# A three-layer conv/attention/expert kernel: DVE's address read, SyncE's bulk loads, V's place and attention's chunk stages are reordered

## The reference

```
x = x + moe0(groupnorm(x))      # 8 experts, top 2; gelu(x w1 + b1) w2 + b2 per expert, and a shared gated FFN
t = t + attention(layernorm(t)) # 12 heads of 16 channels per image
t = t + moe1(layernorm(t))      # 16 experts, top 2; silu(x wg) * (x wu) wd, and a shared one

# attention, per image and head (256 x 256):
att = softmax(q k^T / 4)
att = softmax(att * mask)       # mask 0.5 where row % 64 == column % 64, else 1
out = (att v) w_out + b_out
```

## Time and profile before

| | |
|---|---|
| median of the runs shown | 509.32 us |
| profiled execution | 508.83 us, span 507.0 us, mean granted PE clock 0.97 |
| PE / DVE / ACT / POOL busy | 455.0 / 225.8 / 158.4 / 125.4 us |
| layer 0: routing and shared FFN, expert loop, sums | to 56, 56 to 157, 157 to 181 us |
| Q, K, V; attention; tail and routing | 181 to 211, 211 to 324, 324 to 362 us |
| layer 1's expert loop; sums and output | 362 to 492, 492 to 507 us |
| chain that ended last | PE 76%, DVE 8%, DMA 7%, issue 4% |

### The profile page before, as it was taken

How to read it: one execution, slowest core, us unless ns; L and a number is a source line. 1 busy time by engine, 2 the same in 40 slices (tenths; PEclk the granted TensorE clock), 3 DMA queues, 4 the chain that set the end, 5 groups by cost and what they waited for, 6 DMA issues and landing times.

```text
span 507.0 us, 7727 instructions
## 1 busy us (share of the span) xinstructions
PE 455.0 (90%) x2395; PEld 327.7 (65%) x2396; DVE 225.8 (45%) x597; ACT 158.4 (31%) x394; POOL 125.4 (25%) x136
## 2 busy tenths in 40 slices
PE   0999889999998598799999997799899999999996
PEld 0755456666668587777676766555577777777775
DVE  4465142222221475367878794545253333333322
ACT  2024312121221033348768683312222222222210
POOL 3201144454442000000000000000335455544430
PEclk9999989999999899579999999899999999999999
DMA  8997001111001980000000038093001101110006
GB/s 235 250 340 204 16 25 40 40 34 37 28 16 55 307 346 2 0 1 0 1 3 1 1 77 204 1 258 84 18 25 30 31 26 31 33 37 20 0 2 186
DMA packets 18057, 38.64 MB, mean 76 GB/s; under 512 B 4420, under 2 KB 13892, under 8 KB 17586
## 3 DMA queue, kind: packets, MB, share of 16 engines
q1 hardware_dynamic: 10610, 30.45, 21.0%
q0 software_dynamic: 5280, 6.32, 4.4%
q10 hardware_dynamic: 2144, 1.57, 1.0%
HBM read 35.16 MB, written 7.67 MB: 84 GB/s over the span
## 4 chain that ended last, share of the span: by engine, by line
PE 76%; DVE 8%; DMA 7%; issue 4%; ACT 2%; DVEq 1%; POOL 1%; POOLq 0%; ACTq 0%; SPq 0%
PE bank L1174 16%; PE bank L1189 12%; PE bank L1110 10%; PE bank L1168 5%; PE bank L1359 5%; DVE scratch L995 4%; PE bank L1354 4%; PE bank L1181 3%; PE bank L1312 3%; DMA w_first<-y_rows 3%; PE bank L1150 2%; DMA rows<-xn_rows,slot_tok 2%; PE bank L1096 2%; PE bank L1373 2%; PE bank L1341 2%
## 5 line engine op out<-in xcount | busy, mean ns | idle before, releaser
L1174 PE MATMUL bank<-w_first,rows_t 96*128 x248 | 85.4, 487 | 0.8 <-ACT rows_t L587 0.6
L502 POOL DMA_INDIRECT y_rows<-y,slot_row x54 | 55.4, 1025 | 108.2 <-DVE y L871 58.4
L494 POOL DMA_INDIRECT rows<-xn_rows,slot_tok x56 | 57.4, 1025 | 94.1 <-DVE slot_tok L821 36.9
L1189 PE MATMUL bank<-w_second,hid_t 128*128 x370 | 70.8, 331 | 7.6 <-issue 3.9
L1189 PEld LDWEIGHTS bank<-w_second,hid_t 128*128 128x128 f32 x370 | 59.1, 191 | 10.6 <-issue 10.5
L1174 PEld LDWEIGHTS bank<-w_first,rows_t 96*128 96x128 f32 x248 | 44.6, 190 | 26.2 <-issue 1.5
L655 ACT ACTIVATE scratch<-bank,neg_max 128x256 f32<-128x256 f32 x96 | 44.2, 481 | 8.4 <-PE bank L1341 7.5
L863 DVE TENSOR_TENSOR act_h<-bank,act_g 128x384 f32<-128x384 f32 x31 | 17.3, 557 | 63.8 <-PE bank L1174 63.8
L1168 PE MATMUL bank<-w_first,rows_t 96*128 (+1 forms) x92 | 44.3, 603 | 1.1 <-issue 1.0
L540 POOL COPY act_h<-o_inv 128x256 f32<-128x256 f32 x12 | 4.8, 403 | 154.6 <-DVE o_inv L1005 154.6
L995 DVE SCALAR_TENSOR_TENSOR scratch<-scratch,exp_inv,const 128x256 f32<-128x256 f32 x96 | 41.4, 492 | 0.8
(11 more groups left out here) (175 smaller groups left out, 658.5 us busy)
## 6 DMA issues: line engine op xcount, KB each, us to landing
w_first<-in_gate_up SPq DMA_DIRECT2D x16, 576.0 KB, 11.0
w_second<-in_down SPq DMA_DIRECT2D x1, 4608.0 KB, 25.9
w_first<-in_fc SPq DMA_DIRECT2D x1, 3072.0 KB
w_second<-in_fc SPq DMA_DIRECT2D x1, 3072.0 KB, 28.5
xn_rows<-xn_tok SPq DMA_DIRECT2D x2, 768.0 KB, 10.0
rows<-xn_rows,slot_tok POOLq DMA_INDIRECT x56, 2.6
y_rows<-y,slot_row POOLq DMA_INDIRECT x54, 2.3
w_first<-in_x_t SPq DMA_DIRECT2D x2, 384.0 KB, 5.0
```

What stands on the lines that cost most here:

```text
L494: pool.indirect_dma_start(rows[b % 2][:], None, xn_rows[L.l], bass.IndirectOffsetOnAxis(slot_tok[:, b:b + 1].bitcast(U32), 0), bounds_chec ...
L502: pool.indirect_dma_start(y_rows[L.l], bass.IndirectOffsetOnAxis(slot_row[:, b:b + 1].bitcast(U32), 0), y[b % 2][:], None, bounds_check=TO ...
L1174: ins = pe.matmul(bank[:, 5 + g, 0:I1], rows_t[0:CH, k, :], w(CH, (k * 2 + g) * I1, I1), start=(k == 0), stop=(k == NCH - 1))
L1189: ins = pe.matmul(bank[:, 1, 0:C], hid_t[:, tile(ic)], w(P, ic * C, C), start=(ic == 0), stop=(ic == L.IC - 1))
```

## The change

Four orders change; no arithmetic does.

1. `result`: layer 0's bias address is read into its register ahead of the waits for `y_ps` and `scattered`.
2. SP waits for both parts of both returned rows of layer 0 (`y_in[0]`, `y_in[1]`) before it issues `wo`, the gate/up weights and `down`, instead of for layer 0's last product.
3. PE computes V ahead of the scores of pairs 0 and 1, and waits for Q's and K's parts only behind it; DVE copies V ahead of the two row maxima.
4. In attention the chunk stages of PE stand ahead of `att_transpose(p)`, behind the wait for `p2_ready`, in the order spread, values, sums, project, at lags 3, 1, 2 and 4. Fillers: 2 for pairs 0 to 2, then 1, and none in a step with values or project. ACT's and DVE's loops have 28 steps, and PE's 24 with four more written out, so the last chunks take the same path; on DVE `residual` comes last in a step and `out_norm` and `invert_sums` ahead of `neg_maximum`. In the 4 steps behind the last pair PE has the normalization's transposes and the shared FFN between the stages, and 5 fillers. The shared FFN's (1, 1) moves from `plan[1]` ahead of the second logits, (1, 0) ahead of the second transposes.

The diff, cut to its core:

```diff
+        VALUES, SUMS, SPREAD, PROJECT = 1, 2, 3, 4
+
         def chunk_at(p, lag):
             c = (p - lag + 1) // PAIRS_CHUNK - 1
-            if c == N_CHUNKS - 1 or (p - lag + 1) % PAIRS_CHUNK or c < 0 or c >= N_CHUNKS:
-                return None
-            return c
+            return None if (p - lag + 1) % PAIRS_CHUNK or c < 0 or c >= N_CHUNKS else c
+
+        def image_at(p):
+            c = chunk_at(p, PROJECT)
+            return c // HC if c is not None and c % HC == HC - 1 else None
+
+        STEPS = range(N_PAIRS + PROJECT)
...
-            1: ([(1, 1), (2, 0), "count", (2, 1), "rank", (3, 0), "expert", (3, 1), (4, 0), (4, 1), (5, 0), "slots",
+            1: ([(2, 0), "count", (2, 1), "rank", (3, 0), "expert", (3, 1), (4, 0), (4, 1), (5, 0), "slots",
...
             bring_back(sp, L0, 0)
-            sp.wait_ge(L0.y_ps, NB0)
+            for s in L0.y_in[0:2]:
+                sp.wait_ge(s, 16 * TOPK)
             sp.dma_start(wo, d["wo"]).then_inc(s_attw, 16)
...
-            for p in range(N_PAIRS):
+            for p in STEPS:
                 if p + 2 < N_PAIRS:
                     exp_scores(p + 2)
-                exp_att(p)
-                if chunk_at(p, 1) is not None:
-                    out_copy(chunk_at(p, 1))
-            out_copy(N_CHUNKS - 1)
+                if chunk_at(p, VALUES) is not None:
+                    out_copy(chunk_at(p, VALUES))
+                if p < N_PAIRS:
+                    exp_att(p)
...
             def result(L, b, u, turn):
+                if L.l == 0:
+                    at = dve.value_load(blk_weights[0:1, 2, bass.ds(b, 1)], min_val=0, max_val=(E0 - 1) * C)
                 dve.wait_ge(L.y_ps, b + 1)
...
-            neg_maximum(0)
-            neg_maximum(1)
             dve.wait_ge(filled, 1)
             for n in range(NT // 2):
                 dve.wait_ge(v_ps, n + 1)
...
+            neg_maximum(0)
+            neg_maximum(1)
...
-            for p in range(N_PAIRS):
-                if p == 0:
-                    neg_maximum(2)
-                if (chunk_at(p, 5) or 0) % HC == HC - 1:
-                    residual(chunk_at(p, 5) // HC)
-                attention(p)
+            neg_maximum(2)
+            for p in STEPS:
+                if p < N_PAIRS:
+                    attention(p)
+                if p == N_PAIRS:
+                    ln_stats(0)
+                if p == N_PAIRS + 2:
+                    ln_rows(2, 0)
+                if chunk_at(p, SUMS) is not None:
+                    invert_sums(chunk_at(p, SUMS))
+                if chunk_at(p, SPREAD) is not None:
+                    out_norm(chunk_at(p, SPREAD))
                 if p + 3 < N_PAIRS:
                     neg_maximum(p + 3)
-                if chunk_at(p, 2) is not None:
-                    invert_sums(chunk_at(p, 2))
-                if chunk_at(p, 3) is not None:
-                    out_norm(chunk_at(p, 3))
...
+                if image_at(p) is not None:
+                    residual(image_at(p))
...
-            pe.wait_ge(parts_ready, 2 * QKC)
-            scores(0)
-            scores(1)
             for n in range(NT // 2):
...
                 ins.then_inc(v_ps, 1)
+            pe.wait_ge(parts_ready, 2 * QKC)
+            scores(0)
+            scores(1)
             pe.wait_ge(v_out, NT // 2)

             def att_transpose(p):
-                if p:
-                    pe.wait_ge(p2_ready, p)
-                for _ in range(2 if p else 8):
-                    pe.matmul(bank[:, 4, 0:TOKENS_IMG], ident, mask, start=True, stop=True)
                 pe.wait_ge(att_ready, p + 1)
...
+            def chunk_stages(p):
+                if p:
+                    pe.wait_ge(p2_ready, min(p, N_PAIRS))
+                stages = ((SPREAD, spread_inverses), (VALUES, weigh_values), (SUMS, sums_by_token))
+                for lag, stage_of in stages:
+                    if chunk_at(p, lag) is not None:
+                        stage_of(chunk_at(p, lag))
+                if image_at(p) is not None:
+                    project(image_at(p))
+
+            def keep_busy(n):
+                for _ in range(n):
+                    pe.matmul(bank[:, 4, 0:TOKENS_IMG], ident, mask, start=True, stop=True)
+
+            scores(2)
             for p in range(N_PAIRS):
-                if p == 0:
-                    scores(2)
                 if p + 3 < N_PAIRS:
                     scores(p + 3)
+                chunk_stages(p)
+                if chunk_at(p, VALUES) is None and image_at(p) is None:
+                    keep_busy(2 if p < 3 else 1)
                 att_transpose(p)
-                if chunk_at(p, 2) is not None:
-                    sums_by_token(chunk_at(p, 2))
-                if chunk_at(p, 3) is not None:
-                    spread_inverses(chunk_at(p, 3))
-                if (chunk_at(p, 4) or 0) % HC == HC - 1:
-                    project(chunk_at(p, 4) // HC)
-                if chunk_at(p, 1) is not None:
-                    weigh_values(chunk_at(p, 1))
...
+            chunk_stages(N_PAIRS)
+            keep_busy(2)
+            chunk_stages(N_PAIRS + 1)
+            keep_busy(2)
             norm_transposes(2, 0)
+            chunk_stages(N_PAIRS + 2)
+            keep_busy(1)
             pe.wait_ge(tp_out, NT + 2)
             pe.wait_ge(s_sh1, 32)
             shared(L1, 0, 0)
+            chunk_stages(N_PAIRS + 3)
             shared(L1, 0, 1)
...
+            shared(L1, 1, 0)

             pe.wait_ge(x_new, IMAGES)
             norm_transposes(2, 1)
-            shared(L1, 1, 0)
+            shared(L1, 1, 1)
```

More of the change, by code:

```diff
@@ L872, in result @@
                 else:
-                    at = dve.value_load(blk_weights[0:1, 2, bass.ds(b, 1)], min_val=0, max_val=(E0 - 1) * C)
                     ins = v.tensor_tensor(y[u][:], bank[:, 1, 0:C], fc2_b[:, bass.ds(at, C)], ALU.add)
@@ L1021, in residual @@
                 dve.sem_inc(x_new, 1)
-            for p in range(N_PAIRS):
-                if p == 0:
-                    neg_maximum(2)
-                if (chunk_at(p, 5) or 0) % HC == HC - 1:
-                    residual(chunk_at(p, 5) // HC)
-                attention(p)
+            neg_maximum(2)
[10 more added lines that the diff above has]
+                    out_norm(chunk_at(p, SPREAD))
                 if p + 3 < N_PAIRS:
                     neg_maximum(p + 3)
-                if chunk_at(p, 2) is not None:
-                    invert_sums(chunk_at(p, 2))
-                if chunk_at(p, 3) is not None:
-                    out_norm(chunk_at(p, 3))
-            ln_stats(0)
-            out_norm(N_CHUNKS - 2)
-            invert_sums(N_CHUNKS - 1)
-            ln_rows(2, 0)
-            out_norm(N_CHUNKS - 1)
-            residual(IMAGES - 1)
+                if image_at(p) is not None:
+                    residual(image_at(p))
             ln_stats(1)
@@ L1407, in project @@
                 ins.then_inc(proj_ps, 1)
+            def chunk_stages(p):
[11 more added lines that the diff above has]
+            scores(2)
             for p in range(N_PAIRS):
-                if p == 0:
-                    scores(2)
                 if p + 3 < N_PAIRS:
                     scores(p + 3)
+                chunk_stages(p)
+                if chunk_at(p, VALUES) is None and image_at(p) is None:
+                    keep_busy(2 if p < 3 else 1)
                 att_transpose(p)
-                if chunk_at(p, 2) is not None:
-                    sums_by_token(chunk_at(p, 2))
-                if chunk_at(p, 3) is not None:
-                    spread_inverses(chunk_at(p, 3))
-                if (chunk_at(p, 4) or 0) % HC == HC - 1:
-                    project(chunk_at(p, 4) // HC)
-                if chunk_at(p, 1) is not None:
-                    weigh_values(chunk_at(p, 1))
-            weigh_values(N_CHUNKS - 1)
-            spread_inverses(N_CHUNKS - 2)
-            sums_by_token(N_CHUNKS - 1)
-            spread_inverses(N_CHUNKS - 1)
-            project(IMAGES - 1)
+            chunk_stages(N_PAIRS)
+            keep_busy(2)
+            chunk_stages(N_PAIRS + 1)
+            keep_busy(2)
             norm_transposes(2, 0)
+            chunk_stages(N_PAIRS + 2)
+            keep_busy(1)
             pe.wait_ge(tp_out, NT + 2)
```

## The result

The changed kernel takes 480.28 us (median of 4 runs, 476.89 to 484.92; the kernel before 509.27 beside it), a ratio of 0.942 with a 95% interval of 0.934 to 0.950. The forecast was 483.1. The profiled execution took 480.29 us, its span is 478.5 us. The kernel's four runs differ by the clock that they were granted (mean 0.985 in the fastest, 0.975 in the two in the middle, 0.968 in the slowest), so I compare stretches of traces more than medians.

What follows compares the result with a forecast made beforehand. PE bounds both expert loops, layer 0's often leaving it for DVE, GpSimd and transfers; PE and DVE alternate in attention. 5.1 + 6.0 + 5.4 + 10.4 - 0.7 = 26.2 us less gives 483.1 us; range 478 to 494.

Steps and rivals of the forecast that it cites:

- Part 1: Layer 0's expert loop: reading the bias address ahead of the wait gains 5.1 us, range 3 to 6.5.
- PE's own pace is late next, (8.64 - 8.12) / 2 = 0.26 a block away: Layer 0's expert loop: PE's pace of 8.12 us a pair limits the gain to 3.1 us over six pairs.
- Part 2: Returned rows before attention: bulk loads behind them bring the first QK matmul 6.0 us earlier, range 4 to 6.5.
- Part 3: Way into attention: V ahead of the scores and fewer fillers at step 0, net gain 5.4 us, range 3 to 7.
- V no longer has that wait ... I take full clock: V's 48 matmuls, without the 1.41 us wait for the last K part, take 5.5 us at full clock.
- 4.9, 4.3 and 3.5 us for the first three steps: Attention's first three steps: PE enters at half clock and has full clock from the third on.
- Part 4: Attention from step 3 to 23: the new stage order takes 71.5 us, gain 10.4, bounds 0 and 12.1.
- Rival A: Attention keeps its pace, new hand-over waits or clock falls taking back what the fillers give; 493 us, chance 0.20.
- its waits for sums, spread and project ... go: Attention: DVE's waits for these PE stages vanish, since PE has done them by then; image 21.5 us.
- the 2 us that the prediction named as a sign of being wrong: Attention: the prediction is wrong if DVE still idles over 2 us an image.
- Part 5: Attention's tail: second logits end equally late, about 22 us after step 23; moved work worth nothing, cost 0.7 us.
- 0 to -1.8, one `shared` at half clock: Attention's tail: range of the cost if the hole left on PE costs clock; -0.7 us taken.

Runs made afterwards that it cites:

- b: Kernel before the change, with only GpSimd's order changed: the gather of the block four ahead issued before the finished block's scatter; 500.60 us, ratio 0.980.
- c: Changed kernel with SyncE again waiting for layer 0's last second matmuls, not the returned rows, before the bulk loads; 491.67 us.
- d: Kernel before the change, with only V moved ahead of the first two pairs' scores (PE's order and VectorE's); 506.33 us, ratio 0.994.
- e: Changed kernel with V put back behind the first two pairs' scores, on PE and VectorE; 483.17 us.
- h: Changed kernel without any filler matmuls; 484.33 us, ratio 0.954.
- f: Kernel before the change, stages in old order, with the changed kernel's filler count from step 3 on (7 instead of 40); 514.59 us, ratio 1.013.
- g: Changed kernel with two fillers in every attention step (40 instead of 7 between steps 3 and 23); 499.04 us, ratio 0.980.
- i: Changed kernel with the second shared projection, shared(L1, 1, 1), back behind the second logits; 476.23 us, ratio 0.933.
- j: Changed kernel with five filler matmuls in PE's 2.64 us hole between the second logits and the routing's count; 475.40 us, ratio 0.934.
- k: Changed kernel with gather ahead of scatter, second shared projection back behind the second logits, and 12 fillers ahead of scores(2); 472.33 us, ratio 0.929.
- l: k with one small exponential on ScalarE ahead of its wait for V, for an early table load; 473.64 us.

## Why the prediction came out right, and where it was wrong

**Part 1, mis-sized.** The mechanism held: no sequencer time before the addition, and the last result 0.62 us nearer to PE's end (0.77 to 0.15 us; forecast 0.75). The failed step is "PE's own pace is late next, (8.64 - 8.12) / 2 = 0.26 a block away". The 8.12 a pair, read off two pairs at the end of the loop, was not PE's own: a weight load still waited 0.48 us for gathered rows there once a pair (139.26 in the trace before), and behind it stood 0.37 us of "issue", second matmuls of 1.56 instead of 1.30 and hidden transposes of 0.57 instead of 0.44, 0.76 in all. b takes the pair to 7.49 without touching PE or DVE, and both edits to 7.36, PE's own pace, whose terms stood in the chain. So the six pairs gave 4.6 us (forecast 3.1) and the two at the end 1.4 (forecast 0). Some 2.1 us came from the start of the loop (forecast 0.7): the second pair took 10.53 us before and 8.85 after, the third 8.33 and 7.92, and the clock's dip of 3.41 us that lay there is gone.

**Part 2, right.** No wait for rows at tile 4; the second half landed some 6.6 us behind its issue (at most 6.5 forecast), the first QK matmul came 17.20 us behind the start of the last result (17.6; the forecast's own terms, 172.7 + 0.9 + 2.0, add to 0.2 more). c shows the cause.

**Part 3, right in time of the parts that it worked out, wrong in the cause of one.** V took 5.3 us at 1.00, and counted from the first QK matmul the exponentials started 3.7 us earlier (3.6), step 0 8.2 us earlier (8.3). "V no longer has that wait ... I take full clock" is true of the trace, and c and d show it with late rows; but e has the wait, early rows and full clock too, so V's place is one of two ways to it. What was mis-sized is "4.9, 4.3 and 3.5 us for the first three steps": 3.99, 3.25 and 3.19, 10.43 in all, since the clock was back 2.7 us into step 0 (200.49) and not at the third step. Of the 2 fillers of step 0, too, nearly all stood in idle time: h, without them, is 0.4 us shorter there. And what d and the fall from 8 fillers to 2 give apart are 4.8 us (V, at full clock) and 3.4 (36.41 to 32.98).

**Part 4, right, and as argued.** Even steps 3.52 us (3.45), odd ones 3.19 (3.05), with project 4.71 (4.65), clock 1.00. f and g show that both halves are needed, which the sum assumed by taking PE's and DVE's chains as nearly equal. Rival A fell. But "its waits for sums, spread and project ... go" held only for spread: in an image DVE still waits 1.1 us for sums and 0.8 for project (before 1.8, 1.8, and 0.8 for spread), and it idles 21.66 - 19.49 = 2.17 us, just over the 2 us that the prediction named as a sign of being wrong. PE's loop, which sets the pace, was right without it.

**Part 5, mis-sized.** "0 to -1.8, one `shared` at half clock" failed: in the profiled run the clock, once down, stayed down for 13.65 us of dense matmuls, and this cost 6.46 us. i and j show that it goes with the hole that the part made; h and k show that a hole is neither enough for a fall nor needed for one, and what decides stays open. The rest of the part came out (21.85 us to the logits, forecast 22.1).

## What to carry to other kernels

Take an engine's own pace as the sum of its terms in the chain, not from a stretch that looks free: another loop may still hold it. Where two engines' chains bind almost together, price an edit with its partner; alone each half can be a loss. A hole that costs nothing by itself can cost the clock of all that follows it, in some runs and not in others: fill it, or put waiting work into it, and judge by several runs. If a forecast comes out, compare it part by part; here two large errors cancelled.

## What the runs showed of the hardware

- In the changed kernel's trace 2.64 us of idle time on PE were followed by 13.65 us at 1.2 GHz, with PE busy through all of them; five fillers of 2.4 us in all prevented it (j, four runs). In h 2.65 us of idle time at the same place were followed by full clock, and in k and l the clock fell there for 6.83 and 3.41 us without the hole.
- Steps of scores, 128x128 transposes and values hold 2.4 GHz with no filler at all (70.75 us, mean clock 0.98), but the old order with few fillers, where PE waits 19.3 us for DVE in these steps instead of 6.5, does not (f, mean 0.86).
- V's 48 matmuls ran at 1.2 GHz in the four traces with V behind the scores and the rows late, and at 2.4 GHz in the three with only one of the two (c, d, e).
- The same kernel's runs differ by the clock: the changed kernel 476.9 us at a mean of 0.985 to 484.9 at 0.968, e 476.6 at 0.989 to 487.2 at 0.965. i, j and k, with the holes closed or filled, lie 0.6, 2.1 and 2.0 us apart; but g, with the hole open, only 0.3, so the hole does not explain the spread alone.
- ACT's second half of the returned rows landed 12.05 us behind its issue when `wo`, 4 gate/up loads and `down` were issued within 4 us behind it (c), and some 6.6 when they waited for it; the first half took 4.7 in both.
